# VectorE computes the attention weights of three key tiles in six cross-attention units

## The reference

```python
q = (query @ Wq + bq).reshape(B, Nq, H, D).transpose(0, 2, 1, 3)
k = (key_value @ Wk + bk).reshape(B, Nkv, H, D).transpose(0, 2, 1, 3)
v = (key_value @ Wv + bv).reshape(B, Nkv, H, D).transpose(0, 2, 1, 3)
attn = jnp.einsum('bhqd,bhkd->bhqk', q, k) * scale        # H = 16 heads of D = 8
attn = jnp.clip(attn, -CLAMP, CLAMP)
attn = jax.nn.softmax(attn, axis=-1)
x = jnp.einsum('bhqk,bhkd->bqhd', attn, v).reshape(B, Nq, Cq)
return x @ Wo + bo
```

## Time and profile before

| | us |
|---|---|
| median of 3 runs | 1003.07 (1001.84 to 1008.03) |
| the profiled execution | 1005.74 |
| its span, first to last instruction | 1003.8 |
| PE busy | 875.2 |
| ACT busy | 868.0 |
| DVE busy | 167.5 |
| mean granted clock of PE | 0.982 |

### The profile page before, as it was taken

The page is one execution under the profiler, slowest core; times in us unless marked ns, Lnnn a source line. Parts: engine busy times, 40 slices in busy tenths (PEclk is TensorE's granted clock), DMA queues, the critical chain, the costliest instruction groups (busy, mean ns, idle before and its releaser), DMA issues.

```text
span 1003.8 us, 14820 instructions
## 1 busy us (share of the span) xinstructions
PE 875.2 (87%) x6128; PEld 257.4 (26%) x6128; DVE 167.5 (17%) x432; ACT 868.0 (86%) x664; POOL 9.1 (1%) x33
## 2 busy tenths in 40 slices
PE   6977889998888888888899888888888888899997
PEld 4552322221111111111122211111111111134443
DVE  5764543420000000000013000000000000033212
ACT  4666978999999999999999999999999999933342
POOL 3000000000000000000000000000000000000000
PEclk9987999999999999999999999999998999999999
DMA  4251007211211111111221111112221000020200
GB/s 142 106 184 43 2 17 215 69 32 42 45 41 39 35 35 33 32 39 43 45 41 36 32 32 36 35 34 46 40 44 35 1 1 2 1 86 1 84 10 11
DMA packets 19716, 46.31 MB, mean 46 GB/s; under 512 B 6210, under 2 KB 9388, under 8 KB 19132
## 3 DMA queue, kind: packets, MB, share of 16 engines
q1 hardware_dynamic: 19644, 45.31, 17.7%
HBM read 38.18 MB, written 7.11 MB: 45 GB/s over the span
## 4 chain that ended last, share of the span: by engine, by line
PE 35%; ACT 31%; issue 31%; DVE 2%; DMA 1%; SPq 0%; ACTq 0%; DVEq 0%
ACT probs L710 31%; PE psum L1370 10%; PE psum L1334 6%; PE psum L1590 6%; PE psum L1602 5%; PE psum L1226 1%; PE psum L1266 1%; PE psum L1270 1%; PE psum L1486 1%; DVE turned L929 1%; PE psum L1366 1%; PE psum L1253 1%; PE psum L1472 0%; DMA ctx_region<-in_ctx 0%; PE psum L1210 0%
## 5 line engine op out<-in xcount | busy, mean ns | idle before, releaser
L710 ACT ACTIVATE probs<-psum 128x1536 f32<-128x1536 f32 (+1 forms) x520 | 784.1, 1777 | 30.0 <-PE psum L1334 15.9
L1370 PE MATMUL psum<-probs,v_ctx 128*9 128x512 f32 x3200 | 422.7, 600 | 3.1 <-DVE turned L929 2.7
L1334 PE MATMUL psum<-q_all,k_ring 32*128 32x512 f32 (+1 forms) x1792 | 265.1, 493 | 105.5 <-ACT probs L710 102.5
L1334 PEld LDWEIGHTS psum<-q_all,k_ring 32*128 32x128 f32 x1792 | 102.7, 185 | 501.2 <-ACT probs L710 453.6
L929 DVE STREAM_TRANSPOSE turned<-psum 128x512 f32<-128x512 f32 x16 | 11.5, 717 | 625.9 <-PE psum L1366 609.0
L762 ACT ACTIVATE probs<-psum,b_sb 128x512 f32<-128x512 f32 x64 | 44.0, 687 | 71.8 <-PE psum L1590 71.7
L1370 PEld LDWEIGHTS psum<-probs,v_ctx 128*9 128x9 f32 x3200 | 47.6, 88 | 104.7 <-issue 97.5
L1590 PE MATMUL psum<-xnT,w_region 128*128 128x512 f32 x128 | 65.3, 594 | 1.7 <-issue 1.7
L1602 PE MATMUL psum<-probs,ctx_region 128*128 128x512 f32 x128 | 65.0, 592 | 0.0
L1370 PE MATMUL psum<-probs,v_self 128*9 128x512 f32 (+3 forms) x384 | 41.1, 528 | 2.0 <-DVE probs L950 1.4
L1602 PEld LDWEIGHTS psum<-probs,ctx_region 128*128 128x128 f32 x128 | 24.3, 190 | 30.6 <-issue 30.6
(11 more groups left out here) (144 smaller groups left out, 248.1 us busy)
## 6 DMA issues: line engine op xcount, KB each, us to landing
k_ring<-kc_parts SPq DMA_DIRECT2D x256, 52.0 KB
k_ring<-kc_parts SPq DMA_DIRECT2D x256, 48.0 KB
kc_parts<-kparts_bc SPq DMA_DIRECT2D x8, 512.0 KB, 2.8
probs<-gate_rows SPq DMA_DIRECT2D x4, 1024.0 KB, 5.9
kc_parts<-probs SPq DMA_DIRECT2D x4, 512.0 KB, 2.8
w_region<-in_L_ffn_W SPq DMA_DIRECT2D x1, 2048.0 KB, 9.3
ctx_region<-in_ctx SPq DMA_DIRECT2D x1, 768.0 KB, 8.9
ctx_region<-in_ctx SPq DMA_DIRECT2D x1, 672.0 KB, 7.5
```

Of the source, the lines that this page charges most:

```text
L710: act.activation(probs[:, slot:slot + w, :], psum[:, at:at + w, :], ACT.Exp, scale=SC[ph]).then_inc(L[ph]["exp_done"], 1)
L1334: mm = pe.matmul(into[:, col:col + n_q], keys, q_all[rows, g, hf * HALF + q0:hf * HALF + q0 + n_q], start=True, stop=True)
L1370: mm = pe.matmul(into[:, q0:q0 + w], v_all[:, h, t, :], probs[:, place(ph, at)[1], col:col + w], start=first, stop=last)
```

## The change

In units 1, 2, 3, 5, 6 and 7, the weights of key tiles 0, 13 and 26 are computed by DVE and not by ACT: 6 x 3 x 4 lanes = 72 of the 1600 banks. In these units every second group of four keeps three banks for ACT, and its fourth is one lane of such a tile (a **V group** in what follows, 72 in all). The exponential of a V group is 128x1536. PE still computes its four scores and signals them together.

`vector_lane` makes the weights of one lane with eight DVE instructions of 128x512 each. It rounds the score to an integer by adding a large constant (line 1073), takes the remainder (1075, after which the PSUM bank may be used again: semaphore `taken`), builds the power of two as bits (1079), and evaluates a polynomial in the remainder (1084, 1086 three times, 1087). Each of them waits for the one before. Queries are scaled so that scores count powers of two, and ACT's `Exp` has ln 2 as its scale. The polynomial's leading factor is multiplied into a copy of v (`vector_v`, three small DVE instructions ahead of the phase). The weights go into four fixed buffers, one for each lane, in place of tensors no longer used.

A tile of DVE's is summed in the loop three groups past the one that holds its last lane (`VECTOR_LAG`), after a wait for the semaphore `made`. PE waits for `taken` before it reuses a bank that DVE reads (`taken_before`). The lanes of a unit stand in DVE's program behind the transpose, reciprocal and scaling of the unit before.

Groups are now formed for each unit by itself: each unit starts with a group at banks 0 to 3 (0 to 2 in unit 4). The number of groups is 472 as before. Of them ACT handles 115 as 128x2048, 355 as 128x1536 (72 of these are V groups), and two smaller ones.

```diff
+VECTOR_TILES = (0, 13, 26)
+VECTOR_UNITS = (1, 2, 3, 5, 6, 7)
+VECTOR_LAG = 3
...
+def cross_groups(slot):
+    groups, batches, group_of = [], [], {}
+    def put(banks, at, vector):
+        nonlocal slot
+        w = len(banks) - vector
+        slot = slot if slot + w <= SLOTS else 0
+        for bank in banks:
+            group_of[bank] = len(groups)
+        groups.append((banks, at, slot, vector))
+        slot += w
+    for unit, (half, g, tiles) in enumerate(cross_plan()):
+        scalar = [(r, g, t, half) for t, vector in tiles if not vector for r in range(LANES)]
+        lanes = [(r, g, t, half) for t, vector in tiles if vector for r in range(LANES)]
+        threes, n, fours = BESIDE.get(unit, 0), 0, 0
+        while scalar:
+            size = 3 if threes > 0 else (4, 3)[n % 2]
+            at = 3 * (n % 2) if threes > 0 else 4 * (n % 2)
+            threes -= size
+            if threes <= 0 < threes + size:
+                n = 1
+            vector = size == 4 and bool(lanes) and lanes[0][2] <= scalar[0][2] and fours % 2 == 0
+            fours += size == 4
+            take = min(size - vector, len(scalar))
+            banks, scalar = scalar[:take], scalar[take:]
+            put(banks + [lanes.pop(0)] if vector else banks, at, vector)
+            n += 1
+        assert not lanes
+    for unit, (half, g, tiles) in enumerate(cross_plan()):
+        order = []
+        for t, vector in tiles:
+            ready = max(group_of[r, g, t, half] for r in range(LANES))
+            order.append((ready + (VECTOR_LAG if vector else 0), t, vector))
+        last = max(ready for ready, t, vector in order if not vector)
+        order = sorted((min(ready, last), vector, t) for ready, t, vector in order)
+        for i, (ready, vector, t) in enumerate(order):
+            batches.append((g, half, i == 0, False, t, ready, vector))
+        batches.append((g, half, False, True, None, last, False))
+    return groups, batches, group_of
...
+def taken_before(group):
+    return sum(CROSS_GROUPS[n][3] for n in range(1 + max([m for m in range(group) if meets(1, m, group, 1)], default=-1)))
...
+        vector_p = [v_self[:, :, :, :].rearrange("p h t c -> p (h t c)")[:, r * HALF:(r + 1) * HALF] for r in range(2)] + \
+            [w_quads[:, :, :, :, :, :].rearrange("p w g r j d -> p (w g r j d)")[:, r * HALF:(r + 1) * HALF] for r in range(2)]
+        vector_n, vector_u = x_plain, x_low
+        vector_v = v_gen[:, :, :].rearrange("p t c -> p (t c)")[:, 0:H * len(VECTOR_TILES) * VC]\
+            .rearrange("p (h t c) -> p h t c", h=H, t=len(VECTOR_TILES))
...
+            quad_weights(2, wq_sb[:, :], [sign * QUERY_SCALE for sign in Q_SIGNS], s["wcross_quads"])
...
-                    first, w, at, slot = GROUPS[ph][g]
+                    _, at, slot, _ = GROUPS[ph][g]
+                    w = scalar_banks(ph, g)
                     act.wait_ge(L[ph]["qk_done"], g + 1)
-                    held = before_in(ph, g, 3)
+                    held = before_in(ph, g, 2)
...
+                def vector_lane(tile, r):
+                    _, _, _, _, groups = VECTOR_WORK[tile]
+                    n = tile * LANES + r
+                    def powered(ins):
+                        powers[0] += 1
+                        ins.then_inc(L[1]["power"], 1)
+                        dve.wait_ge(L[1]["power"], powers[0])
+                    scores = bank(GROUPS[1][groups[r]][1] + scalar_banks(1, groups[r]))
+                    dve.wait_ge(L[1]["qk_done"], groups[r] + 1)
+                    dve.tensor_scalar(vector_n, scores, ROUND, None, ALU.add).then_inc(L[1]["rounded"], 1)
+                    dve.wait_ge(L[1]["rounded"], n + 1)
+                    dve.scalar_tensor_tensor(vector_u, vector_n, ROUND, scores,
+                                             ALU.subtract, ALU.subtract).then_inc(L[1]["taken"], 1)
+                    dve.wait_ge(L[1]["taken"], n + 1)
+                    powered(dve.tensor_scalar(vector_n.bitcast(I32), vector_n, 127.0 - ROUND, 2.0 ** 23, ALU.add, ALU.mult))
+                    if tile and r == 0:
+                        unit_before, _, _, t_before, _ = VECTOR_WORK[tile - 1]
+                        dve.wait_ge(L[1]["pv_batches"], vector_batch(unit_before, t_before))
+                    weights = vector_p[r]
+                    powered(dve.scalar_tensor_tensor(weights, vector_u, POWERS[4], vector_u, ALU.add, ALU.mult))
+                    for c in (3, 2, 1):
+                        powered(dve.scalar_tensor_tensor(weights, weights, POWERS[c], vector_u, ALU.add, ALU.mult))
+                    dve.scalar_tensor_tensor(weights, weights, POWERS[0], vector_n, ALU.add, ALU.mult)\
+                        .then_inc(L[1]["made"], 1)
+                    dve.wait_ge(L[1]["made"], n + 1)
                 while n < len(ends):
+                    if ph == 1:
+                        for tile, work in enumerate(VECTOR_WORK):
+                            if work[0] == n:
+                                for r in range(LANES):
+                                    vector_lane(tile, r)
                     unit(n)
...
+            for n, t in enumerate(VECTOR_TILES):
+                ins = dve.tensor_scalar(vector_v[:, :, n, :], v_ctx[:, :, t, :], LEAD, None, ALU.mult)
+            step(ins)
...
+                        if t is None:
+                            mm = pe.matmul(into, v_ctx[:, h, KT, :], ptail[:, hf * HALF:(hf + 1) * HALF],
                                            start=False, stop=last)
-                            continue
-                        at, (_, t, _, q0, w, col) = places[r]
-                        mm = pe.matmul(into[:, q0:q0 + w], v_all[:, h, t, :],
-                                       probs[:, place(ph, at)[1], col:col + w], start=first, stop=last)
+                        elif vector:
+                            mm = pe.matmul(into, vector_v[:, h, VECTOR_TILES.index(t), :], vector_p[r],
+                                           start=first, stop=last)
+                        else:
+                            mm = pe.matmul(into, v_ctx[:, h, t, :], probs[:, slot_of((r, g, t, hf)), :],
...
-                        held = before_in(ph, group + 2, 2)
+                        held = before_in(ph, group + 2, 1)
                         if held > group:
                             pe.wait_ge(L[ph]["exp_done"], held + 1)
+                        if ph == 1 and taken_before(group + 2):
+                            pe.wait_ge(L[1]["taken"], taken_before(group + 2))
                         score_group(ph, group + 2)
...
+                        if ph == 1 and batches[n][6]:
+                            vector_sums += 1
+                            pe.wait_ge(L[1]["made"], vector_sums * LANES)
                         sum_batch(n)
```

More of the change, by code:

```diff
@@ L142 @@
+SELF_BANK_LIST, SELF_BATCHES = self_plan()
+SELF_GROUPS, NEXT_SLOT = score_groups(SELF_BANK_LIST, (3, 3), 0)
+CROSS_GROUPS, CROSS_BATCHES, CROSS_GROUP_OF = cross_groups(NEXT_SLOT)
 GROUPS = (SELF_GROUPS, CROSS_GROUPS)
-GROUP_OF = [[n for n, (_, w, _, _) in enumerate(groups) for _ in range(w)] for groups in GROUPS]
+SELF_AT = [(n, i) for n, (here, _, _, _) in enumerate(SELF_GROUPS) for i in range(len(here))]
+VECTOR_WORK = [(unit, g, half, t, [CROSS_GROUP_OF[r, g, t, half] for r in range(LANES)])
+               for unit, (half, g, tiles) in enumerate(cross_plan()) for t, vector in tiles if vector]
```

147 lines of the change are left out of this document (86 added, 61 removed).

## The result

The kernel before ran in 1004.8 us (median of 4), the changed one in **1032.9 us**: 1.027 times as long, with a 95% interval of 1.024 to 1.031. The forecast was 1015, with a range of 998 to 1032. The sign was right, the size was too small by more than the whole forecast loss.

The account below looks back on a forecast made before the run. ACT was taken as the bound, with PE close behind and DVE free. Terms -30.2 + 12.6 + 27.5 + 1.4 = +11.3 us gave 1017.0 against the profiled execution, 1015 as the median; range 998 to 1032.

Parts of the forecast that it names:

- six entries into units with lanes: Boundaries leading into units with DVE lanes: 5.08 us of ACT standing each, 30.5 in all, +27.5 net.
- entry into unit 4: Boundary into the unit without a DVE lane: ACT stands 1.82 us in all, +1.4 net.
- PE's clock: Rival in cross-attention: longer PE idle times could lower its clock from 1.00; upper side of the range, no size or chance.
- The entry: At each boundary into a unit with lanes, ACT loses 0.93, 0.07, then 4.08 us waiting for DVE's first lane.
- Doubled batches: PE loops summing a DVE tile besides another: ACT stands 0.70 us at each of 18 tiles, +12.6.
- The stops before: ACT's stops at unit boundaries in the old kernel: 5 x 0.38, and the first 0.70 and 0.38, 3.0 us.
- ACT's gain: 72 ACT groups in cross-attention shrink from four banks to three, 1.77 to 1.35 us each: -30.2 us.
- DVE's lane: Eight DVE instructions at 0.72 us make a lane of 5.8, equal to ACT's pace, so costing nothing.
- DVE is in time: Rival at boundaries: first lane's bank is free before PE asks, ACT stands under 3 us; 990 us, chance 0.09.
- DVE's lane is the pace: Rival inside units: a DVE lane takes 6.2 us, 0.4 more than ACT's 5.8; 1030 us, chance 0.14.
- Gain and losses cancel: Rival over cross-attention: a bank saves 0.52, a doubled batch costs 0.38, net -2; 1001 us, chance 0.27.

Follow-up runs that it names:

- pauses filled: Changed kernel plus 6 and 12 dummy PE matmuls before its waits for the shared banks and for DVE's bank at unit boundaries: 1007.4 us, 1.004.
- lane of five steps: Changed kernel without the three middle polynomial steps (line 1086) of each DVE lane, so its weights are not the reference's: 1031.3 us, 1.027.
- best form: Changed kernel with groups running on over unit boundaries, DVE's tiles 3, 16 and 29, and V groups whose four lanes all differ: 981.5 us, 0.977.

## Why the prediction was wrong in size, step by step

The terms in us, each beside what the traces show; the last column is the kernel with the pauses filled (6 and 12 matmuls). The forecast's sum stood for 1014.4 us as a median, which I wrote as 1015.

| term | forecast | changed kernel | pauses filled |
|---|---|---|---|
| ACT's exponentials, busy | -30.2 | -26.9 | -29.1 |
| stops at DVE's 18 tiles | +12.6 | +5.8 | +5.8 |
| in five units, ACT waits once for a batch | 0 | +1.6 | +1.6 |
| six entries into units with lanes | +30.5 | +44.6 | +28.6 |
| entry into unit 4 | +1.8 | +3.0 | +1.4 |
| other stops of cross-attention | 0 | +3.3 | +1.5 |
| the stops before, in place of which these stand | -3.4 | -5.8 | -5.8 |
| stops of ACT in self-attention | 0 | +0.5 | -4.0 |
| ACT's waits in the experts | 0 | +2.1 | -0.1 |
| sum | +11.3 | +28.2 | -0.1 |
| span | | +28.1 | +0.3 |

- **The step that failed** is the last of the rivals: "PE's clock ... I have no row for how often; it belongs to the upper side of the range." It was left without a price, and it is what separates the two right columns: 44.6 - 28.6 = 16.0 at the six entries, 1.6 at unit 4 and 1.8 elsewhere in cross-attention, some 19 us, and 2.2 of ACT's exponentials that stood alone (a record is 1.45 behind a wait, where the pace is 1.35). The remaining 4.5 in self-attention and 2.2 in the experts lie where no kernel here changes an instruction. There too the clock differs between the two executions that were profiled: 0.92 and 0.97 from 66 to 224 us, 0.83 and 1.00 in the 10 us in which the experts' first results come. The lane of five steps, which has no filler, was also profiled at 0.97 there, with stops of 20 us in self-attention as in the filled kernel. So these 6.7 us aren't the filler's doing, but belong to the execution. The medians differ by 24.5.
- Rows for its price were there. I read the clock in a stretch in which it stayed up. Inside unit 6 of the kernel before, between DVE's transposes of 703.29 and 794.17, PE has pauses of 1.20 us like this first one, and behind the second the clock is down:

```profile
749.41 0.50 PE L1334 MATMUL psum<-q_all,k_ring 32*128 32x512 f32 x4 [1.20 <-ACT probs L710]
...
761.87 0.80 PE L1334 MATMUL psum<-q_all,k_ring 32*128 32x512 f32 x4 [1.20 <-ACT probs L710]
762.59 1.89 PE L1370 MATMUL psum<-probs,v_ctx 128*9 128x512 f32 x8
764.42 0.80 PE L1334 MATMUL psum<-q_all,k_ring 32*128 32x512 f32 x3
...
765.26 1.45 ACT L710 ACTIVATE probs<-psum 128x1536 f32<-128x1536 f32 x1 [0.34 <-PE psum L1334]
...
767.82 1.88 ACT L710 ACTIVATE probs<-psum 128x2048 f32<-128x2048 f32 x1 [1.11 <-PE psum L1334]
```

```profile
762.00:768.00 6.00, 6.00 (x31) 1.12 (x35) 0.00 (x0) 4.55 (x4) 0.00 (x0) 0.50 0.00 0
```

  The loop is 764.42 - 761.87 = 2.55, the stop 1.11. Of some forty pauses of this length before, three are followed by the lower level (297.55, 649.01 and 761.87), so the old trace has its price, but it doesn't say how often it comes, and it has no pause of over 1.3 us there. My own steps gave PE pauses of about 3 us at six boundaries (5.96 to 8.99). A batch of 1.83 in place of 0.98, a tail of 1.5 in place of 1.0, and two or three loops of 1.11 behind them make 3.6 to 4.7 us per entry, 22 to 28 in all if the clock fell at every one, and 1037 to 1043: a rival of its own. Measured were 16.0.
- *The other terms were too dear*, and that is luck for the number. With the pauses filled the sum is -0.1 and the time 1007, not 1015; what the clock cost beyond that was partly hidden by this error of 11 us in the sum.
- *The entry* was right in every step but for the clock: V group 0.82 against 0.93, DVE's wait 3.86 against 4.08, PE released by L1075 as said.
- *Doubled batches*: 0.48 against 0.70, in the main since two batches in a row take 1.83 and not 1.96, and only 12 instead of 18. At a unit's third tile no V group follows any more, and the batch lies beside a group of four: there 1.77 covers it. I had read "the loop ahead has just scored a V group" from two tiles and used it for three.
- *The stops before*: I used the 0.38 of one boundary for five. The trace of before has 0.38 at two of them, 0.31 at one and none at two.
- *ACT's gain*: 26.9 against 30.2, and 29.1 with the pauses filled. The pace is as forecast: 16 exponentials in 23.30 are (23.30 - 1.5) / 15 = 1.45 each, with three of 1.35 to one of 1.77.
- *DVE's lane*: 355.90 - 350.40 = 5.5 against 5.8, the end of L1087 included. The 0.43 of line 1079 is the cheaper SBUF-to-SBUF instruction with one source that the Trainium skill, "VectorE: DVE Perf Modes", tier table, describes; by its rule the lane was 5.5, and the trace agrees. It changed no verdict, as the five-step lane shows.
- *The rivals*: "DVE is in time" is refuted: the cheapest of the six entries cost 5.5. "DVE's lane is the pace" came nearest in its time, 1030, by a mechanism that isn't there. "Gain and losses cancel" was wrong here, though it is what happens at the upper clock level, 1007.

Not settled: why ACT's exponential finds its buffer late once in five of the six units (0.32), and what decides behind which pause the clock falls: in the changed kernel eleven of the twelve pauses of 1.6 to 3.1 us at boundaries are followed by 0.50 within some 2 us, the one that ends at 812.85 is not.

## What to carry to other kernels

A pause of the engine that isn't the bound is not only its length: price what the engine's work costs at the lower clock, from any rows of the old trace that show it, and not only from a stretch at the upper one. Where work is handed to an idle engine, look first at what that engine has to finish before it (here a unit's end), and place the first piece behind that: the choice of tiles 0 or 3 was worth 38 us, the whole offload in its best form 23. And before a step is moved back, ask who waits for the buffers it holds.
